# Three score banks in the last two second attentions, and two pairs of banks for the first attention's maxima

## What is computed

```python
# layer 0: "first attention", H, D = 16, 64
logits = einsum('bqhd,bkhd->bhqk', q, k) / sqrt(64)
probs  = softmax(where(tril, logits, neg))
out    = einsum('bhqk,bkhd->bqhd', probs, v)
# layer 1: "second attention", H = 16, hd = 8
q, k   = rope3d(heads(x @ Wq + bq)), rope3d(heads(x @ Wk + bk))
attn   = softmax(einsum('bhqd,bhkd->bhqk', q, k) * hd ** -0.5)
ctx    = einsum('bhqk,bhkd->bhqd', attn, v)
```

## The kernel before

| banks | first attention | second attention |
|---|---|---|
| 0, 1 (`banks0`) | maxima scores of two heads | maxima scores, one of two pairs in turn |
| 2, 3 (`banks1`) | transposed scores of two heads | transposed scores, in turn |
| 4 | P·V | P·V |
| 5 | mailbox of the chain (`side`) | batches 0 and 1: third bank for transposed scores; batches 2 and 3: mailbox |
| 6, 7 (`banks3`) | q, k, v projections and the two rows of maxima | the other pair for maxima scores |

## Time and profile before

### The profile page before, as it was taken

One profiled execution on the slowest core, in us unless ns is written; L12 is line 12 of the kernel. 1 busy time (PEld: TensorE's weight loads), 2 busy tenths in 40 slices (PEclk: granted clock), 3 DMA queues, 4 the chain that ended last, 5 costly groups with the idle time before them and its releaser, 6 DMA issues.

```text
span 2920.3 us, 39514 instructions
## 1 busy us (share of the span) xinstructions
PE 2297.5 (79%) x14753; PEld 920.2 (32%) x14757; DVE 1671.7 (57%) x2893; ACT 1277.4 (44%) x2289; POOL 700.9 (24%) x490
## 2 busy tenths in 40 slices
PE   3989997988677778788767778789877777578776
PEld 2434443444121233444212133344422222111112
DVE  3454456466767356655576735755666664666624
ACT  1333432433467534233256754324334455256552
POOL 0655554344200024333310014334420000000000
PEclk9999998999899889899789999989988887778889
DMA  2000010011100001001110000101111000200000
GB/s 74 14 22 22 21 40 14 11 35 47 45 15 1 11 4 50 11 11 33 54 37 15 1 13 11 40 11 36 37 50 38 1 1 15 87 1 1 8 1 8
DMA packets 81200, 69.14 MB, mean 24 GB/s; under 512 B 46673, under 2 KB 62801, under 8 KB 80497
## 3 DMA queue, kind: packets, MB, share of 16 engines
q1 hardware_dynamic: 81008, 66.60, 8.3%
HBM read 57.58 MB, written 8.98 MB: 23 GB/s over the span
## 4 chain that ended last, share of the span: by engine, by line
PE 59%; DVE 23%; ACT 9%; issue 6%; SPq 3%; DMA 1%; ACTq 0%; DVEq 0%
PE banks L800 57%; DVE pmax L2235 5%; ACT ring L1657 5%; DVE part_max L1835 4%; SPq L626 2%; ACT room L1472 1%; DVE ntmp L1784 1%; PE banks L929 1%; DVE tmp L1739 1%; DVE h L1803 1%; DVE stats L1791 1%; DVE ntmp L1739 1%; DVE room L1993 1%; DVE x_b L1739 1%; DVE oT L1856 1%
## 5 line engine op out<-in xcount | busy, mean ns | idle before, releaser
L764 POOL TENSOR_TENSOR p_sum<-p_sum,ring 128x1024 f32<-128x1024 f32 (+3 forms) x320 | 547.2, 1710 | 907.8 <-PE banks L800 478.1
L2235 DVE TENSOR_REDUCE pmax<-banks 128x2 f32<-128x1024 f32 x512 | 607.9, 1221 | 227.4 <-PE banks L800 225.0
L800 PE MATMUL banks<-ring,v 128*9 128x512 f32 (+4 forms) x2816 | 593.4, 619 | 0.0
L1835 DVE TENSOR_REDUCE part_max<-banks 128x2 f32<-128x1024 f32 (+3 forms) x384 | 368.0, 958 | 387.4 <-PE banks L800 385.7
L800 PE MATMUL banks<-qT,kT 64*128 64x512 f32 (+4 forms) x2048 | 471.1, 523 | 85.8 <-DVE pmax L2235 54.9
L1657 ACT ACTIVATE ring<-banks 128x512 f32<-128x512 f32 x768 | 415.9, 595 | 243.3 <-PE banks L800 242.7
L1429 ACT ACTIVATE ring<-banks 128x1024 f32<-128x1024 f32 (+3 forms) x320 | 245.9, 768 | 461.0 <-PE banks L800 459.7
L800 PE MATMUL banks<-oT 64*128 64x512 bf16 x1024 | 221.1, 427 | 118.9 <-ACT ring L1657 99.9
L800 PEld LDWEIGHTS banks<-qT,kT 64*128 64x128 f32 (+1 forms) x2048 | 146.7, 168 | 372.9 <-issue 152.4
L800 PE MATMUL banks<-p_sum,v 128*9 128x512 f32 (+1 forms) x768 | 222.5, 658 | 34.0 <-DVE oT L1856 33.0
L800 PE MATMUL banks<-k_bf,q_bf 64*128 64x512 bf16 (+3 forms) x768 | 134.7, 342 | 123.3 <-DVE part_max L1835 122.7
(11 more groups left out here) (268 smaller groups left out, 2600.9 us busy)
## 6 DMA issues: line engine op xcount, KB each, us to landing
inv_bc<-softmax_inverses SPq DMA_DIRECT2D x64, 256.0 KB, 4.0
w_qk<-in_L_attn_w_qkv SPq DMA_DIRECT2D x64, 64.0 KB, 2.1
low<-in_L_ffn_attention_mask SPq DMA_DIRECT2D x4, 1024.0 KB, 6.1
stage<-rope_constants SPq DMA_DIRECT2D x4, 1024.0 KB, 5.0
x_b<-in_L_attn_x SPq DMA_DIRECT2D x4, 512.0 KB, 5.1
w_v<-in_L_attn_w_qkv SPq DMA_DIRECT2D x32, 64.0 KB, 2.1
stage<-in_L_ffn_w SPq DMA_DIRECT2D x8, 256.0 KB, 6.0
out<-x_b SPq DMA_DIRECT2D x16, 128.0 KB, 1.8
```

Source lines behind the costliest of these rows:

```text
L764: pool.tensor_tensor(sv, sv, ring0[SLOT[m]][:, :, 0:HALF - lo], ALU.add).then_inc(sem("added"), 1)
L800: return pe.matmul(dst, lhsT, rhs, start=start, stop=stop)
L1835: dve.reduce_max(part_max[:, :, t, c], banks[0][:, :, 0:w], AX).then_inc(sem("row_max"), 1)
L2235: dve.reduce_max(pmax1[:, :, g, t, c], banks[(0, 3)[USE1[b]["max", m] % 2]][:, :, :], AX).then_inc(sem("row_max1"), 1)
```

## The change

The change has two parts.

1. First attention: the maxima items alternate between `banks0` and `banks3` by `MAX_PAIR`; each waits for the last reader of its own banks (`MAX_BEFORE`, or v's copies, or a copied row). The second row of maxima goes to bank 0 instead of bank 7.
2. Second attentions of batches 2 and 3: transposed scores use three banks (2, 3, 5) as in the other batches. The chain steps there write the first bank of `banks0` or `banks3` and have a turn among the uses of the pairs. ScalarE's chain step comes ahead of the row copy and the context copy of a step instead of behind.

The diff:

```diff
--- before.py
+++ after.py
@@ -54,6 +54,11 @@
 OWN_MAX_AT = {0: (10,), 1: (11,)}
 FIRST_MAX = 10
 
+MAX_PAIR = (0, 3, 0, 3, 0, 3, 0, 0, 0, 3, 0, 3)
+MAX_BEFORE = (None, None, 0, 1, 2, 3, 4, 6, 7, None, 8, 9)
+ROW_BANK = (6, 0)
+ROW_BEHIND = (5, 10)
+
 RING = 3
 SLOT = {}
 RING_BEFORE = {}
@@ -81,7 +86,7 @@
 OUT_AT = {26: 0, 28: 1}
 FIRST_PAIR_AT = CTX_AT and max(CTX_AT) + 1
 assert US + 2 < LEAD < 2 * US
-ST1_BANKS = [(2, 3, 5)] * (B - 2) + [(2, 3)] * 2
+ST1_BANK = (2, 3, 5)
 TERMS = [(0, "h", "h"), (8, "h", "m"), (16, "m", "h"), (24, "h", "l"), (34, "m", "m"), (42, "l", "h")]
 HM = 64
 M_ROW = 32
@@ -115,11 +120,11 @@
             order.append(("ctx", CTX_AT[k]))
         if k in OUT_AT and b + 1 < B:
             order.append(("out", OUT_AT[k]))
+        for step in LATE_STEPS[b].get(k, ()) if b in LATE_STEPS else ():
+            if step[0][0] != "~":
+                order.append(("side", step))
     return order
 
-
-USES1 = [uses_of_pairs1(b) for b in range(B)]
-USE1 = [{use: n for n, use in enumerate(order)} for order in USES1]
 
 
 MOD0 = ["mod0", "~gates0"]
@@ -196,6 +201,9 @@
 
 
 LATE_STEPS = {B - 2: late_steps_of(B, 29, STEPS1 - 1), B - 1: late_steps_of(B + 1, 1 - LEAD, 90)}
+USES1 = [uses_of_pairs1(b) for b in range(B)]
+USE1 = [{use: n for n, use in enumerate(order)} for order in USES1]
+LATE_IN = {step: b for b in LATE_STEPS for steps in LATE_STEPS[b].values() for step in steps if step[0][0] != "~"}
 
 
 def side_order():
@@ -438,7 +446,19 @@
 
         banks = [ctx.enter_context(nc.psum_tensor(f"banks{n}", [P, 2, HALF], F32)) for n in range(4)]
         bank = [banks[n // 2][:, n % 2, :] for n in range(8)]
-        side = bank[5]
+
+        class Mailbox:
+            at = bank[5]
+
+            def of(self, step):
+
+                b = LATE_IN.get(step)
+                self.at = bank[5] if b is None else banks[(0, 3)[USE1[b]["side", step] % 2]][:, 0, :]
+
+            def __getitem__(self, key):
+                return self.at[key]
+
+        side = Mailbox()
 
         den_dram = nc.dram_tensor("softmax_sums", [B * NP, 4, HALF], F32).ap()
         inv_dram = nc.dram_tensor("softmax_inverses", [B * NP, 4, HALF], F32).ap()
@@ -461,6 +481,7 @@
             return sems[name]
 
         def filled(eng, step):
+            side.of(step)
             eng.wait_ge(sem("side_mm"), SIDE[step] + 1)
 
         def read_out(eng, step):
@@ -809,8 +830,11 @@
 
             def side_free(step):
 
+                side.of(step)
                 if SIDE[step]:
                     pe.wait_ge(sem("side_out"), SIDE[step])
+                if step in LATE_IN:
+                    pair_free1(LATE_IN[step], "side", step)
 
             half = [slice(0, HD0), slice(HD0, P)]
 
@@ -824,7 +848,7 @@
                     if k:
                         pe.wait_ge(sem("q_evac"), 2 * n + c + 1)
                     elif n:
-                        pe.wait_ge(sem("mrow_evac"), 2 * n - 1 + c)
+                        pe.wait_ge(sem("row_max"), NI * n)
                     mm(bank[6 + c][:, :], w_qk[k][:, :], hT[:, c * HALF:(c + 1) * HALF]).then_inc(sem("qk_proj"), 1)
 
             def project_v(n):
@@ -840,23 +864,30 @@
                 t, c, w = MAX_ITEMS[m]
                 pe.wait_ge(sem("qb_cast"), 2 * n + t // 4 + 1)
                 pe.wait_ge(sem("kb_cast"), 2 * n + c + 1)
-                if n or m:
-                    pe.wait_ge(sem("row_max"), NI * n + m)
+                if MAX_BEFORE[m] is not None:
+                    pe.wait_ge(sem("row_max"), NI * n + MAX_BEFORE[m] + 1)
+                elif m == 0 and n:
+                    pe.wait_ge(sem("mrow_evac"), 2 * n)
+                elif m == 1:
+                    pe.wait_ge(sem("v_evac"), 2 * n + 2)
+                elif m == 9:
+                    pe.wait_ge(sem("mrow_evac"), 2 * n + 1)
                 diag = c == t // 4
+                dst = banks[MAX_PAIR[m]]
                 for s in range(2):
-                    last = mm(bank[s][:, 0:w], q_bf[half[s], t * P:(t + 1) * P], k_bf[half[s], c * HALF:c * HALF + w], stop=not diag)
+                    last = mm(dst[:, s, 0:w], q_bf[half[s], t * P:(t + 1) * P], k_bf[half[s], c * HALF:c * HALF + w], stop=not diag)
                 if diag:
                     for r in range(2):
                         for s in range(2):
-                            last = mm(bank[s][:, w - P:w], eye_halves[half[s], r, :], mask_q[half[s], r, :], start=False, stop=r == 1)
+                            last = mm(dst[:, s, w - P:w], eye_halves[half[s], r, :], mask_q[half[s], r, :], start=False, stop=r == 1)
                 last.then_inc(sem("s_mm"), 1)
 
             def max_to_row(n, c):
 
                 pe.wait_ge(sem("neg_max"), 2 * n + c + 1)
-                pe.wait_ge(sem("v_evac"), 2 * n + c + 1)
+                pe.wait_ge(sem("row_max"), NI * n + ROW_BEHIND[c] + 1)
                 for t in range(4):
-                    last = mm(bank[6 + c][:, t * P:(t + 1) * P], max_cols[:, 4 * c + t, :], eye_bf[:, :])
+                    last = mm(bank[ROW_BANK[c]][:, t * P:(t + 1) * P], max_cols[:, 4 * c + t, :], eye_bf[:, :])
                 last.then_inc(sem("mrow_mm"), 1)
 
             def st_item(n, m):
@@ -1198,6 +1229,8 @@
                         pe.wait_ge(sem("mrow1"), 2 * (UNITS * b + by + 1))
                     elif used == "ctx":
                         pe.wait_ge(sem("ctx1"), (UNITS - 1) * b + by + 1)
+                    elif used == "side":
+                        read_out(pe, by)
                     else:
                         pe.wait_ge(sem("res_a"), 2 * b + by + 1)
                 return banks[(0, 3)[n % 2]]
@@ -1236,12 +1269,11 @@
                     if b < B - 1:
                         read_out(pe, ("den", pairs - 1))
                     else:
-                        read_out(pe, ("v1_1", b))
-                st_banks = ST1_BANKS[b]
-                if n >= 2 and (n % 2 == 0 or len(st_banks) == 2):
+                        read_out(pe, ("ctx7", b - 1))
+                if n % 2 == 0 and n >= 2:
                     pe.wait_ge(sem("expd1"), NI1 * b + n - 1)
                 rows = slice((a % 2) * HM, (a % 2) * HM + K_ALL)
-                mm(bank[st_banks[n % len(st_banks)]][:, :], ks[u // C][rows, a // 2, j * P:(j + 1) * P], qs[u // C][rows, a // 2, (u % C) * HALF:(u % C + 1) * HALF]).then_inc(sem("st1_mm"), 1)
+                mm(bank[ST1_BANK[n % 3]][:, :], ks[u // C][rows, a // 2, j * P:(j + 1) * P], qs[u // C][rows, a // 2, (u % C) * HALF:(u % C + 1) * HALF]).then_inc(sem("st1_mm"), 1)
 
             def pv1_items(b, k):
 
@@ -1401,7 +1433,7 @@
 
             def max_rows(n, c):
                 act.wait_ge(sem("mrow_mm"), 2 * n + c + 1)
-                copy(m_row[n % 2][:, c * HALF:(c + 1) * HALF], bank[6 + c][:, :]).then_inc(sem("mrow_evac"), 1)
+                copy(m_row[n % 2][:, c * HALF:(c + 1) * HALF], bank[ROW_BANK[c]][:, :]).then_inc(sem("mrow_evac"), 1)
 
             def sums_out(n):
 
@@ -1654,14 +1686,14 @@
                             act.wait_ge(sem("pv1"), NI1 // GH * b + n // GH - 1)
                         elif n == 0 and b:
                             act.wait_ge(sem("pv1"), NI1 // GH * b)
-                        act.activation(ring1[n % 8], bank[ST1_BANKS[b][n % len(ST1_BANKS[b])]][:, :], ACT.Exp, scale=SCALE).then_inc(sem("expd1"), 1)
+                        act.activation(ring1[n % 8], bank[ST1_BANK[n % 3]][:, :], ACT.Exp, scale=SCALE).then_inc(sem("expd1"), 1)
+                if b in LATE_STEPS:
+                    for step in LATE_STEPS[b].get(k - 1, ()):
+                        side_step(steps, step)
                 if k + LEAD in ROWS_AT:
                     max_rows1(b, ROWS_AT[k + LEAD])
                 if k + 2 in CTX_AT:
                     o1_raw(b, CTX_AT[k + 2])
-                if b in LATE_STEPS:
-                    for step in LATE_STEPS[b].get(k - 1, ()):
-                        side_step(steps, step)
 
             def first_pair(n, k):
                 if k == 0:
@@ -1832,7 +1864,7 @@
             def row_max(n, m):
                 t, c, w = MAX_ITEMS[m]
                 dve.wait_ge(sem("s_mm"), NI * n + m + 1)
-                dve.reduce_max(part_max[:, :, t, c], banks[0][:, :, 0:w], AX).then_inc(sem("row_max"), 1)
+                dve.reduce_max(part_max[:, :, t, c], banks[MAX_PAIR[m]][:, :, 0:w], AX).then_inc(sem("row_max"), 1)
 
             def final_max(n, c):
```

## The result

The changed kernel takes 2814.05 us (median of 4 runs, 2807.84 to 2820.81), the kernel before 2921.49 beside it: ratio 0.9633, 95% interval 0.9594 to 0.9672. Two later comparisons gave 0.9655 (0.9631 to 0.9679) and 0.9668 (0.9646 to 0.9689). The forecast was 2862, the range 2828 to 2918. The direction was right, the size too small by 48 us.

What follows compares the result with a forecast made beforehand. TensorE, busy 79%, was taken to bound the kernel, waiting for VectorE's maxima reductions and, in the last two second attentions, ScalarE's exponentials. From 2922.12 us, -42 - 45 + 23 + 4 = -60 gave 2862 us, range 2828 to 2918.

Steps and rivals of the forecast that it cites:

- Part one: First attention: two pairs of banks shorten TensorE's waits for the maxima's reductions; -42 us, bounds -20 and -80.
- Part two: Second attentions of batches 2 and 3: a third score bank ends split score matmuls; -45 us, bounds -25 and -60.
- only 0.2 comes back: Near the end, ScalarE does two exponentials in 1.09 us, then stands 0.20 for TensorE, limiting a split step's gain.
- Part three: Last two second attentions: chain steps' turns cost +23 us (bounds 0, +60); row and context copies awaiting readouts, +4.
- the list: Last two second attentions: 64 turns beginning too early for the new rule, 31.4 us in batch 2, 28.7 in batch 3.
- the flat half: Turns in the last two second attentions: half of the 46 us left on the list taken as cost, +23.
- The forecast's own signs: Last two second attentions: more waiting for pmax, less for exponentials; wrong if pmax waits grow by over 45 us.
- The sum leaves the clock as it is: Whole kernel: no term for TensorE's granted clock, 0.82 and 0.83 in the last two second attentions.
- The clock's rival: Last two second attentions: clock rises to 0.90, 35 us more are won, 2827 us; chance 0.08.
- A chain step costs a whole turnaround: TensorE stands through a reduction at each of 69 chain steps: 1.8 us each, +124 against -87, 2959 us; chance 0.05.
- The waits come back: Only the first attention's short waits, some 20 us, are won; parts two and three cancel: 2902 us; chance 0.22.
- The clock falls: First attentions drop to a clock of 0.82, costing 117 us more: 2979 us; chance 0.02.

Runs made afterwards that it cites:

- the turns' run: Kernel before with chain steps in the maxima's banks with own turns and ScalarE's turned order, still two score banks: 2912.19 us, ratio 0.9972; again 2920.51, 0.9994.
- no_own_turn: Changed kernel, but a chain step in the last two second attentions writes the next use's pair, which waits for its readout: 2873.65 us, ratio 0.9827.
- maxima_single: Changed kernel, but second attentions of batches 2 and 3 put all maxima on banks0 and all other uses on banks3: 2911.72 us, ratio 0.9966.
- filler: As the turns' run, plus two unread matmuls into unused bank 5 in every second step: 2934.34 us, ratio 1.0036.

## Why the prediction was right, and where it failed

- **Part one, -42: right.** -33 by the run of that part alone, -41 by the stages of the changed kernel. Which waits go and which stay was as counted (59.7 us left); the share that passes was half by the run alone and nearer two thirds by the stages.
- **Part two, -45: right in its mechanism, somewhat small.** The third bank takes away every split step, and is worth 57 us, between the bound of -60 and the value taken; that includes what the clock gave, which rose with it from 0.85 and 0.85 to 0.90 and 0.87. Near the end, "only 0.2 comes back" was still too much. ScalarE repeats four exponentials in 2.37 us against two in 1.29, 0.10 us a step, not at the 1.1 that was forecast, since TensorE's 0.21 now comes at every second step:

```profile
2722.70 1.08 ACT L1689 ACTIVATE ring<-banks 128x512 f32<-128x512 f32 x2 [0.21 <-PE banks L821]
2723.78 1.08 ACT L1689 ACTIVATE p_sum<-banks 128x512 f32<-128x512 f32 x2
2725.07 2.16 ACT L1689 ACTIVATE ring<-banks 128x512 f32<-128x512 f32 x4 [0.21 <-PE banks L821]
```

- **Part three, +27: this is the step that failed.** Measured: -9 for ScalarE's turned order and about +4 for the turns, so -5. Its +23 for the turns was mis-sized by 19 us and its +4 for the order had the wrong sign, by 13 us. The turned order was priced as a cost of 4 and as a relief of five rows on the list; it is a gain even with no turns at all, presumably because TensorE's next chain step waits for that readout. And the list was taken from a trace in the old order: of its 60.1 us the prediction kept 46, the new order leaves 35.4. That is the smaller part of the miss, since half of 35.4 would still be +18. The other part is the flat half: 90 of 172 passed, 46 of 54, and 4 of 35, so the share is no constant. The forecast's own signs, pmax waits up by less than 45 and those for the exponentials down, came as written, +19.4 and -12.9.
- **"The sum leaves the clock as it is": the second failure.** It rose in just the two stages where it was low. What that is worth can be read where one and the same program ran the same stage at two clocks. Second attention of batch 1 in the two runs of the order alone, whose edit doesn't reach it:

```profile
1485.60:1728.30 242.70, 178.52 (x1238) 47.92 (x1238) 144.45 (x177) 158.68 (x282) 4.81 (x5) 0.89 0.07 19
```

```profile
1486.40:1719.30 232.90, 168.98 (x1238) 45.98 (x1238) 144.47 (x177) 158.68 (x282) 4.80 (x5) 0.94 0.07 20
```

  By the formula above 53 us at 1.2 GHz against 28: 9.8 us for 25, or 0.38 us each. The second attention of batch 2 in another run of the changed kernel took 307.3 us at 0.85 instead of 303.0 at 0.90: 4.3 for 32, or 0.14 each. In the last two second attentions the change brought the time at 1.2 GHz from 221 us to 127. By these two prices that is 13 to 36 of the 71 us won there, an estimate. The times on record give a narrower one. Over the 62 executions of the kernel before in the three later comparisons, the time at 1.2 GHz (583 to 645 us, 612 on average, by the clock of the whole program) and the time (2914 to 2934 us) rise together, 0.28 us for each us at 1.2 GHz (correlation 0.92). Over the 14 of the changed kernel (526 us on average) it is 0.34 (0.96). At these prices the 86 us less at 1.2 GHz are 24 to 29 us of the 97 to 107, an estimate too. They don't come on top of the terms above: the gains of the third bank and of the turns' run hold their share of it. That parts two and three came out as they did is shown by their runs; the clock was not switched by itself.
- **The rivals.** The clock's rival (0.08, 2827 us) had 0.90 for both stages and 35 us for it; measured were 0.90 and 0.87 (0.85 and 0.86 in the other execution), and by the prices above some 25 us. It came nearer than the forecast, but it isn't the whole: 2862 less 25 is 2837. It stood apart from the forecast, as if the clock rose only by chance. By the prices above it belonged into the sum: waits and split steps taken from stages at 0.82 take time at 1.2 GHz with them. The two runs that put waits back show the same backwards. `no_own_turn` had 0.86 and 0.81:

```profile
2125.80:2452.80 327.00, 225.75 (x1431) 74.77 (x1430) 201.33 (x395) 181.69 (x343) 2.35 (x1) 0.86 0.08 23
2510.90:2796.50 285.60, 201.01 (x1170) 45.12 (x1171) 166.38 (x245) 176.72 (x344) 0.00 (x0) 0.81 0.01 3
```

  that is 200 us at 1.2 GHz against the 127, on a list of only 54 us of waits. At 0.14 to 0.38 that makes 10 to 28 of its +46. "A chain step costs a whole turnaround" (+124 for 69 steps) is refuted by the turns' +4. "The waits come back" needed parts two and three to cancel; they gave 68. "The clock falls" did not happen: the first attentions have 0.94, 0.90 and 0.91 where they had 0.95, 0.89 and 0.92.
- The sum of the steps as measured: -33 for part one, -9 for the order, +4 for the turns, -57 for the third bank: -95, against -97 to -107 for the whole and -60 as forecast. So part three makes 32 us of the difference and the third bank 12, of which part one takes 9 back.

What stays open: why the 35 us of the turns cost 4 while 54 us of `no_own_turn` cost 46. The clock went the other way in the two, and which is cause and which effect was not separated. By the executions on record the turns take 22 us less at 1.2 GHz than the order alone (597 against 620), `no_own_turn` 46 more than the changed kernel beside it, `maxima_single` 85 more. At 0.3 us each, an estimate, the three lists without the clock give 11 of 35, 32 of 54 and 64 of 172: nearer to one another, but no common share. A run with the turns but ScalarE's old order, which would price the order once more, can't be had: TensorE would wait, ahead of a row's matmuls, for the readout that ScalarE does only after copying that row.

## What to carry to other kernels

A list of "would have to wait" has to be made on the order that the change will have, not on the old one; make that reordering alone, trace it, and list again. What share of such a list passes to the end is not known ahead: here it was 4 of 35, 90 of 172 and 46 of 54 us. When two matmuls share the array by halves and one is held back, look for the loss in the busy time, not in the idle time. In a stage whose granted clock is well under 1, don't leave the clock out of the sum: price it from executions of the same code at different clocks, the more the better, and add it with the sign of the waits that the change takes away or brings.

## What the runs showed of the hardware beyond that

- The granted clock of a stage differs between executions of the same code. The second attention of batch 1 had 0.89 and 0.94 (242.7 and 232.9 us) in two executions of one kernel; that of batch 0 had 0.90 and 0.94 (239.0 and 232.4 us) in the changed kernel and in `maxima_single`, which doesn't differ up to there. In a comparison by stages such a difference looks like an effect.
- Going round more banks didn't lower the clock here. With the third score bank it was 0.85 to 0.90 in the last two second attentions, with two 0.82 to 0.87 where no filler was added. The Trainium skill, "TensorE: Matmul & The Clock Gate", section "A second HAM failure mode: psum-queue depth-cycling", tells of a kernel that cycles through PSUM banks in each iteration and whose clock swings for it; these runs don't show that.
- Extra matmuls raised the clock from 0.85 to 0.90 in one stage and from 0.85 to 0.86 in the other, and made them 7 and 13 us longer.
